# A one-core convolution kernel: the tap coefficients reordered by small copies instead of a matmul, and the start-up work dealt out anew

## The chip, the cores and the metric

One core of a Trainium2 chip runs the kernel. The metric is the device time of one execution in microseconds (us), lower is better, taken as the median of several executions. The engines are TensorE (PE for its matmuls, PEld for its weight loads), VectorE (DVE), ScalarE (ACT), GpSimd (POOL) and SyncE (SP, which here only issues transfers). Each engine works through its own queue in order; they meet only at semaphores.

## The reference

The input x is 8 images of 32 channels, 64 by 64, in float32. It is normalised per channel and image (32 groups of one channel). The four pixels of each 2 by 2 square become four channel blocks, 128 channels in all, in the order (row parity, column parity) = 00, 01, 10, 11. Three depthwise convolutions of width 1, 3 and 5 give 384 feature channels, `w_proj` (128 by 384) mixes them into 128, these are put back into the 2 by 2 squares, and x is added.

```
xd    = concat(x[:, :, 0::2, 0::2], x[:, :, 0::2, 1::2], x[:, :, 1::2, 0::2], x[:, :, 1::2, 1::2])   # x normalised
feats = concat(dwconv(xd, w1, 1), dwconv(xd, w3, 3), dwconv(xd, w5, 5))
y     = einsum('bchw,oc->bohw', feats, w_proj[:, :, 0, 0])
out   = x + un-deinterleave(y)
```

## The kernel before

The 25 taps of the widest convolution fall into an inner square of 9 and a ring of 16. For an inner tap the three convolutions and the projection are folded into one effective 128 by 128 weight: `weff[n] = w5(n) * wp5^T + w3(n) * wp3^T`, and for the centre also `w1 * wp1^T`. These run on PE. Each weight and each image is split into a high half that PE's fast float32 form holds exactly (`whi`, `HI`) and a remainder (`wlo`, `LO`), and each image takes three passes over its nine taps: `whi` by `HI`, `wlo` by `HI`, `whi` by `LO`, 18 matmuls each of up to 512 columns. The ring runs on the other engines: DVE accumulates its taps in `ACC` (L645, L649), ACT makes further products in `PROD` (L476) and POOL adds them into `RING_SUM` (L343); DVE joins the two in `F` (L661), and PE multiplies `F` by `wpT`, the transposed third part of w_proj (L778, for the last image L788). A last stage adds x and stores. The images follow each other without a gap, and each engine's order is written out by hand.

The change touches the start, in which weights and the statistics of image 0 are made ready:

- The partitions hold the channels in a permuted order (column parity before row parity). w_proj lands in `wp_sb`; ACT permutes its three parts, last one first (L408, semaphore `permuted`); PE transposes them with a permuted identity, `ident_ph` (L795), and ACT copies the third part to `wpT` (L412).
- The 35 coefficients of each channel (25 of w5, 9 of w3, 1 of w1) land in `w_sb` in the reference's order. PE multiplies them by `ident_ph` (L698), which permutes the partitions, and ACT copies the result to `coef` (L414 for the first 34, L494 for w1's).
- The effective weights: ACT scales taps 0 to 2, and after its first HI piece taps 3 and 4 (L420); POOL scales taps 5 to 8 (L358); DVE adds w3's part of each (L600) and w1's part of tap 8 (L631). POOL casts taps 0 to 2 to `whi` (L365), DVE taps 3 to 5 and 6 to 8 (L608); POOL makes `wlo` in three steps (L374).
- The statistics of image 0: DVE takes them in quarters from `XS` (L552), spreads them (L613); PE sums over partitions (`sum_parts`, L705); DVE aggregates (L557) and adds epsilon (L559); POOL raises to the power -1/2 (L312, `inv_std`); DVE makes the bias `nbias` (L564, `part_bias`).
- With these, ACT makes the even columns of the first 17 rows of `HI` of image 0 (L428) and DVE the odd ones (L623). ACT goes on with the other rows and then with `G`, the plain normalised image (L438), on which the ring starts.
- PE runs matmuls on zeros before its work, `WARM[0]` of 256 columns and `WARM[1]` of 512 (L691). Image 0's first pass goes in chunks of three taps; a bank is half an image. It needs `hi_top` (both pieces of HI) and each chunk's `whi`.

Of the kernel before, what the change touches and what calls it, by code (L numbers as in the profile page):

```python
# [6 lines left out]
ACT = mybir.ActivationFunctionType  # L7
# [6 lines left out]
P = 4 * C  # L14
# [36 lines left out]
WARM = (20, 5)  # L51
WARM_COLS = 256
CHUNK = 3
CHUNKS = N_INNER // CHUNK
ACT_SCALED = 5
# [45 lines left out]
def build(nc, x, w1, w3, w5, wp, out):  # L101
    with ExitStack() as ctx:  # L102
# [6 lines left out]
        def sem(name):  # L109
            return ctx.enter_context(nc.semaphore(name))  # L110
# [42 lines left out]
        COEF_PS = SMALL[:, 200:200 + N_COEF]  # L153
# [7 lines left out]
        wp_loaded, w_loaded, w1_loaded = sem("wp_loaded"), sem("w_loaded"), sem("w1_loaded")  # L161
        coef_ready, coef_copied = sem("coef_ready"), sem("coef_copied")
# [83 lines left out]


# [36 lines left out]
        def _(pool):  # L284
# [24 lines left out]
            def inv_std(n, a, b):  # L309
                pool.wait_ge(mhalf_ready, 1)  # L310
                pool.wait_ge(stat_step, n)
                pool.tensor_tensor(rstd[:, a:b], vare[:, a:b], mhalf[:, a:b], ALU.pow).then_inc(rstd_done, 1)  # L312
# [44 lines left out]
            def scale_w5(n):  # L357
                pool.tensor_scalar(weff[:, n, :], wpT[:, :], of5(INNER[n]), None, ALU.mult).then_inc(pool_scaled, 1)  # L358

            inv_std(1, 0, 1)  # L360
            pool.wait_ge(wpT_ready, 1)
            pool.wait_ge(coef_copied, 1)
            scale_w5(ACT_SCALED)
            pool.wait_ge(weff_step, CHUNK)
            pool.tensor_copy(whi[:, 0:CHUNK, :], weff[:, 0:CHUNK, :]).then_inc(whi0_ready, 1)  # L365
            for n in range(ACT_SCALED + 1, N_INNER):
                scale_w5(n)
            for k in range(CHUNKS):
                taps = slice(k * CHUNK, (k + 1) * CHUNK)
                if k == 0:  # L370
                    pool.wait_ge(whi0_ready, 1)
                else:
                    pool.wait_ge(whi_ready, k)
                pool.tensor_tensor(wlo[:, taps, :], weff[:, taps, :],  # L374
                                   whi[:, taps, :].bitcast(F32), ALU.subtract).then_inc(wlo_ready, 1)
# [24 lines left out]
        def _(act):  # L400
            load_parts(act, 0, 512, 1024, xs_loaded[1])
            act.dma_start(w_sb[:, 0:W3_AT], w5.rearrange("c a h w -> c (a h w)")).then_inc(w_loaded, 16)
            act.dma_start(w_sb[:, W3_AT:W1_AT], w3.rearrange("c a h w -> c (a h w)")).then_inc(w_loaded, 16)
# [8 lines left out]
            act.activation(wpT[:, :], WT_PS[:, 2 * P:3 * P], ACT.Copy).then_inc(wpT_ready, 1)  # L412
            act.wait_ge(coef_ready, 1)
            act.activation(coef[:, 0:W1_AT], COEF_PS[:, 0:W1_AT], ACT.Copy).then_inc(coef_copied, 1)  # L414
            act.wait_ge(wpT_ready, 1)
            act.wait_ge(coef_copied, 1)

            def scale_w5(n0, n1):
                for n in range(n0, n1):
                    act.activation(weff[:, n, :], wpT[:, :], ACT.Copy,  # L420
                                   scale=of5(INNER[n])).then_inc(w5_scaled, 1)

            scale_w5(0, CHUNK)
# [68 lines left out]
            scale_w5(CHUNK, ACT_SCALED)  # L492
            act.wait_ge(coef_ready, 2)
            act.activation(coef[:, W1_AT:N_COEF], COEF_PS[:, W1_AT:N_COEF], ACT.Copy).then_inc(coef_copied, 1)  # L494
# [29 lines left out]
        def _(dve):  # L524
# [29 lines left out]
            def part_variance(b):  # L554

                dve.wait_ge(spread_summed, b + 1)
                dve.bn_aggr(agg1[:, b, :], SPREAD_PS[b]).then_inc(agg1_done, 1)  # L557
                dve.wait_ge(agg1_done, b + 1)
                dve.tensor_scalar(vare[:, b:b + 1], agg1[:, b, 1:2], EPS, None, ALU.add).then_inc(stat_step, 1)  # L559
# [44 lines left out]
            def cast_w(k):  # L604
# [9 lines left out]
                              mask[:, :, None].to_broadcast([P, PARTS, STATS]), ALU.mult).then_inc(spread_done, 1)  # L614
            part_variance(0)
            dve.wait_ge(wt_ready, 1)
            dve.wait_ge(coef_copied, 1)
            part_bias(0)
            add_w3(0, 1, 2)
# [6 lines left out]
            add_w3(3, 4, 5)  # L626
# [3 lines left out]
            dve.wait_ge(coef_copied, 2)  # L630
# [54 lines left out]
        def _(pe):  # L685
# [11 lines left out]
            def coefficients(c0, c1):  # L697
                nc.tensor.matmul(COEF_PS[:, c0:c1], ident_ph[:, :], w_sb[:, c0:c1],  # L698
                                 start=True, stop=True).then_inc(coef_ready, 1)

            def sum_parts(b):
                pe.wait_ge(spread_done, b + 1)
                if b == 0:
                    pe.wait_ge(stat_const, PARTS + 1)
                nc.tensor.matmul(SPREAD_PS[b], same[:, :], spread[:, b, :, :].rearrange("p k s -> p (k s)"),  # L705
                                 start=True, stop=True).then_inc(spread_summed, 1)
# [83 lines left out]

            sum_parts(0)
            pe.wait_ge(ident_permuted, 1)
            for n, k in enumerate((2, 1, 0)):
                pe.wait_ge(permuted, n + 1)
                mm = nc.tensor.transpose(WT_PS[:, k * P:(k + 1) * P], wp_ph[:, k, :], ident_ph[:, :])  # L795
            mm.then_inc(wt_ready, 1)
            pe.wait_ge(w_loaded, 32)
            coefficients(0, W1_AT)
# [3 lines left out]
            pe.wait_ge(w1_loaded, 16)  # L802
            pe.wait_ge(coef_copied, 1)
            coefficients(W1_AT, N_COEF)
# [26 lines left out]
```

## Time and profile before

| | |
|---|---|
| median of 3 executions | 135.5 us (135.26 to 136.7) |
| the profiled execution | 135.7 us, of which the profile's span is 133.9 us |
| busy in the span | PE 124.9 us (93%), DVE 125.0 (93%), POOL 119.9 (90%), ACT 110.3 (82%) |
| granted TensorE clock | 0.986 of full speed over the span |

The span runs from the first to the last instruction of the profiled execution; 1.8 us of the execution lie outside it. A busy engine is not yet a late one: what sets the end is seen from the chain of waits and from the order of time in the stage that is changed.

### The profile page before, as it was taken

How to read it: one execution, taken by the hardware profiler on the slowest of the kernel's cores; microseconds unless marked ns; L12 is line 12 of the kernel's file. 1: busy time of each engine (PE TensorE's matmuls, PEld its weight loads, DVE VectorE, ACT ScalarE, POOL GpSimd, SP SyncE). 2: the span in 40 equal slices, each digit the busy share in tenths (PEclk: the TensorE clock that was granted, in tenths of full speed). 3: DMA queues.
4: the chain of work that ended last, by engine and by line, in shares of the span. 5: the costliest groups of instructions: out<-in, count | busy, mean ns of one | idle time of the engine just before them, and what ended most of it. 6: DMA issues, size and time to landing. Idle time of an engine off the chain costs nothing.

```text
span 133.9 us, 1668 instructions
## 1 busy us (share of the span) xinstructions
PE 124.9 (93%) x514; PEld 96.8 (72%) x514; DVE 125.0 (93%) x234; ACT 110.3 (82%) x116; POOL 119.9 (90%) x92
## 2 busy tenths in 40 slices
PE   6968999999999999999999999999999999999910
PEld 6955788888886887688886888688877688578700
DVE  6679999999979999999999999999999999999960
ACT  2389979999999999999999999999999999160010
POOL 6269879999999999999999999999999999999970
PEclk9999999999999999999999999999999999999995
DMA  4999999880044008097979873989299919897876
GB/s 136 260 250 201 207 209 201 169 167 0 5 81 81 0 0 161 5 117 95 187 115 117 155 168 39 91 144 190 30 100 134 186 37 115 91 110 145 182 159 143
DMA packets 35944, 16.68 MB, mean 125 GB/s; under 512 B 34144, under 2 KB 34272, under 8 KB 35552
## 3 DMA queue, kind: packets, MB, share of 16 engines
q0 software_dynamic: 1488, 6.93, 38.8%
q1 hardware_dynamic: 32784, 9.11, 35.6%
q10 hardware_dynamic: 1664, 0.54, 1.7%
q8 instruction: 4, 0.07, 0.2%
q14 instruction: 4, 0.03, 0.1%
HBM read 5.46 MB, written 4.19 MB: 72 GB/s over the span
## 4 chain that ended last, share of the span: by engine, by line
POOL 62%; issue 16%; DVE 12%; PE 4%; POOLq 1%; ACT 1%; ACTq 0%
POOL RING_SUM L343 56%; DVE ACC L649 4%; POOL X L393 3%; PE YP L691 3%; POOL LO L330 2%; DVE st L546 2%; DVE weff L600 2%; DVE whi L608 1%; POOLq L102 1%; DVE ACC L645 1%; DVE stp L552 1%; DVE HI L623 1%; PE YP L795 1%; POOL rstd L312 0%; POOL wlo L385 0%
## 5 line engine op out<-in xcount | busy, mean ns | idle before, releaser
L343 POOL TENSOR_TENSOR RING_SUM<-RING_SUM,PROD 128x900 f32<-128x900 f32 (+1 forms) x45 | 93.0, 2072 | 3.4
L649 DVE SCALAR_TENSOR_TENSOR ACC<-G,coef,ACC 128x480 f32<-128x480 f32 (+3 forms) x132 | 82.4, 742 | 0.0
L476 ACT ACTIVATE PROD<-G,coef 128x900 f32<-128x900 f32 (+1 forms) x45 | 44.5, 1051 | 0.0
L723 PE MATMUL YP<-HI,wlo 128*128 128x512 f32 (+1 forms) x146 | 38.1, 412 | 0.0
L723 PE MATMUL YP<-HI,whi 128*128 128x512 f32 (+1 forms) x146 | 36.2, 398 | 1.7 <-DVE HI L623 1.2
L723 PE MATMUL YP<-LO,whi 128*128 128x512 f32 (+1 forms) x146 | 36.0, 398 | 0.0
L723 PEld LDWEIGHTS YP<-HI,wlo 128*128 128x128 f32 x146 | 27.5, 189 | 8.6 <-issue 2.9
L723 PEld LDWEIGHTS YP<-HI,whi 128*128 128x128 f32 x146 | 27.2, 189 | 8.7 <-DVE HI L623 1.3
L723 PEld LDWEIGHTS YP<-LO,whi 128*128 128x128 f32 x146 | 27.5, 189 | 6.7 <-issue 0.5
L438 ACT ACTIVATE G<-X,nbias,rstd 64x1024 f32<-64x1024 f32 x16 | 21.1, 1321 | 1.2 <-DVE nbias L564 0.9
L459 ACT ACTIVATE Y<-YP 64x1024 f32<-64x1024 f32 x14 | 15.4, 1097 | 3.4 <-PE YP L778 3.1
L778 PE MATMUL YP<-F,wpT 128*128 128x512 f32 x28 | 13.3, 596 | 0.0
L645 DVE TENSOR_SCALAR ACC<-G,coef 128x512 f32<-128x512 f32 x16 | 11.5, 781 | 0.0
L661 DVE TENSOR_TENSOR F<-ACC,RING_SUM 128x512 f32<-128x512 f32 (+1 forms) x18 | 10.7, 672 | 0.0
L467 ACT ACTIVATE RING_SUM<-G,coef 128x1024 f32<-128x1024 f32 x8 | 9.2, 1145 | 0.1
L778 PEld LDWEIGHTS YP<-F,wpT 128*128 128x128 f32 x28 | 5.2, 189 | 4.3 <-issue 3.4
L447 ACT ACTIVATE HI<-G 128x1024 fp32r<-128x1024 f32 x7 | 7.4, 1062 | 0.2
L449 ACT ACTIVATE LO<-HI 128x1024 fp32r<-128x1024 f32 x7 | 7.4, 1062 | 0.2
L546 DVE BATCH_NORM_STATS2 st<-X 128x6 f32<-128x512 f32 x12 | 7.4, 681 | 0.0
L691 PE MATMUL YP<-LO 128*128 128x256 f32 (+1 forms) x25 | 6.1, 423 | 1.2 <-DVE LO L526 1.2
L513 ACT ACTIVATE Y<-YP 64x256 f32<-64x256 f32 x2 | 0.8, 406 | 7.2 <-PE YP L788 7.2
L330 POOL DMA_DIRECT2D LO<-G x7 | 6.4, 914 | 0.0
(69 smaller groups left out, 66.4 us busy)
## 6 DMA issues: line engine op xcount, KB each, us to landing
LO<-G POOLq DMA_DIRECT2D x7, 527.5 KB, 5.3
X<-in_x_dram SPq DMA_DIRECT2D x14, 256.0 KB, 5.5
X<-Y POOLq DMA_DIRECT2D x6, 512.0 KB, 7.3
out_dram<-X SPq DMA_DIRECT2D x12, 256.0 KB, 4.5
XS<-in_x_dram SPq DMA_DIRECT2D x1, 512.0 KB, 6.1
out_dram<-X SPq DMA_DIRECT2D x4, 128.0 KB, 2.2
X<-in_x_dram SPq DMA_DIRECT2D x2, 136.0 KB, 4.4
XS<-in_x_dram SPq DMA_DIRECT2D x1, 256.0 KB, 3.3
```

The costliest lines, as they stand in the source:

```text
L343: pool.tensor_tensor(dst, dst, prod(b, k), ALU.add).then_inc(prod_added, 1)
L438: act.activation(g_image(b, r0, r1)[HALF * j:HALF * (j + 1)], rows[:, :, :, j], ACT.Identity, bias=nbias[p0:p0 + HALF, col(b):col(b) + 1], ...
L459: act.activation(Y[p0:p0 + HALF, b // 2 % 2, :, :, j], YP[HALF * j:HALF * (j + 1), b % AREAS, :].rearrange("p (h w) -> p h w", w=PW), ACT. ...
L467: act.activation(RING_SUM[:, b % SUMS, :, :], g_tap(b, POOL_OF[b][0], True), ACT.Copy, scale=of5(POOL_OF[b][0])).then_inc(first_prod, 1)
L476: act.activation(prod(b, k), g_tap(b, POOL_OF[b][k + 1]), ACT.Copy, scale=of5(POOL_OF[b][k + 1])).then_inc(prod_ready, 1)
L546: dve.bn_stats(st[:, t, q, :], rows).then_inc(bn_done, 1)
L645: dve.tensor_scalar(ACC[:, h * BANK_ROWS:(h + 1) * BANK_ROWS, :], half_tap(b, tap, h, True), of5(tap), None, ALU.mult).then_inc(acc_half[h ...
L649: dve.scalar_tensor_tensor(half_part(ACC, tap, h), half_tap(b, tap, h), of5(tap), half_part(ACC, tap, h), ALU.mult, ALU.add).then_inc(acc_ ...
L661: dve.tensor_tensor(F[:, b % 2, rows.start * PW:rows.stop * PW].rearrange("p (h w) -> p h w", w=PW), ACC[:, rows, :], RING_SUM[:, b % SUMS ...
L691: nc.tensor.matmul(YP[:, 0, 0:n], zeros[:, 0:P], zeros[:, 0:n], start=True, stop=True)
L723: mm = nc.tensor.matmul(dst, w[:, n, :], src, start=start, stop=False, skip_group_check=True)
L778: mm = nc.tensor.matmul(YP[:, b % AREAS, cols], wpT[:, :], F[:, b % 2, cols], start=False, stop=True, skip_group_check=True)
```

## The change

- `w_sb` is no longer permuted on PE. DVE copies w5's 25 columns in four blocks of 32 partitions to `coef`, then w3's nine in four blocks; POOL copies w1's column in four blocks, each of which waits for the one before. Three semaphores (`coef5`, `coef3`, `coef1`) take the place of two. PE's two coefficient matmuls and ACT's two copies of them are gone.
- PE transposes the third part of w_proj ahead of `sum_parts`, into the bank `SMALL`, and the other two behind it. ACT can copy `wpT` after the first.
- ACT scales taps 0 to 6, all ahead of its first HI piece; POOL scales taps 7 and 8.
- DVE adds w3 to taps 0 and 1 before `part_variance(0)`, to 2 and 3 before `part_bias(0)`, to 4 and 5 after its HI piece. POOL scales its first tap before it waits for the variance, and copies w1's column between its last tap and the first `wlo`.
- `WARM[0]` is 17 instead of 20.

```diff
-WARM = (20, 5)
+WARM = (17, 5)
-ACT_SCALED = 5
+ACT_SCALED = 7
+        def in_order(c0, c1, block):
+            src = (block % 2) * 2 + block // 2
+            return coef[C * block:C * (block + 1), c0:c1], w_sb[C * src:C * (src + 1), c0:c1]
...
 # POOL
-            inv_std(1, 0, 1)
             pool.wait_ge(wpT_ready, 1)
-            pool.wait_ge(coef_copied, 1)
+            pool.wait_ge(coef5, 4)
             scale_w5(ACT_SCALED)
+            inv_std(1, 0, 1)
             pool.wait_ge(weff_step, CHUNK)
             pool.tensor_copy(whi[:, 0:CHUNK, :], weff[:, 0:CHUNK, :]).then_inc(whi0_ready, 1)
             for n in range(ACT_SCALED + 1, N_INNER):
                 scale_w5(n)
+            pool.wait_ge(w1_loaded, 16)
+            for block in range(PARTS):
+                if block == 0:
+                    pool.wait_ge(pool_scaled, N_INNER - ACT_SCALED)
+                else:
+                    pool.wait_ge(coef1, block)
+                to, of = in_order(W1_AT, N_COEF, block)
+                pool.tensor_copy(to, of).then_inc(coef1, 1)
+            pool.wait_ge(coef1, PARTS)
...
 # ACT
             act.wait_ge(wt_ready, 1)
-            act.activation(wpT[:, :], WT_PS[:, 2 * P:3 * P], ACT.Copy).then_inc(wpT_ready, 1)
-            act.wait_ge(coef_ready, 1)
-            act.activation(coef[:, 0:W1_AT], COEF_PS[:, 0:W1_AT], ACT.Copy).then_inc(coef_copied, 1)
+            act.activation(wpT[:, :], SMALL[:, 0:P], ACT.Copy).then_inc(wpT_ready, 1)
             act.wait_ge(wpT_ready, 1)
-            act.wait_ge(coef_copied, 1)
+            act.wait_ge(coef5, 4)
-            scale_w5(0, CHUNK)
+            scale_w5(0, ACT_SCALED)
...
             high_half(0, TOP, 0, hi_top)
-            scale_w5(CHUNK, ACT_SCALED)
-            act.wait_ge(coef_ready, 2)
-            act.activation(coef[:, W1_AT:N_COEF], COEF_PS[:, W1_AT:N_COEF], ACT.Copy).then_inc(coef_copied, 1)
...
 # DVE
+            dve.wait_ge(w5_loaded, 16)
+            for block in range(PARTS):
+                to, of = in_order(0, W3_AT, block)
+                dve.tensor_copy(to, of).then_inc(coef5, 1)
+            dve.wait_ge(w3_loaded, 16)
+            for block in range(PARTS):
+                to, of = in_order(W3_AT, W1_AT, block)
+                dve.tensor_copy(to, of).then_inc(coef3, 1)
+            dve.wait_ge(wt_ready, 2)
+            dve.wait_ge(coef3, PARTS)
+            add_w3(0, 1)
             part_variance(0)
-            dve.wait_ge(wt_ready, 1)
-            dve.wait_ge(coef_copied, 1)
+            add_w3(2, 3)
             part_bias(0)
-            add_w3(0, 1, 2)
             dve.wait_ge(stats_ready, 1)
...
-            add_w3(3, 4, 5)
+            add_w3(4, 5)
             cast_w(1)
             add_w3(6, 7, 8)
             dve.wait_ge(weff_step, N_INNER)
-            dve.wait_ge(coef_copied, 2)
+            dve.wait_ge(coef1, PARTS)
...
 # PE
+            pe.wait_ge(ident_permuted, 1)
+            transpose(2, SMALL[:, 0:P]).then_inc(wt_ready, 1)
             sum_parts(0)
-            pe.wait_ge(ident_permuted, 1)
-            for n, k in enumerate((2, 1, 0)):
-                pe.wait_ge(permuted, n + 1)
-                mm = nc.tensor.transpose(WT_PS[:, k * P:(k + 1) * P], wp_ph[:, k, :], ident_ph[:, :])
-            mm.then_inc(wt_ready, 1)
-            pe.wait_ge(w_loaded, 32)
-            coefficients(0, W1_AT)
+            transpose(1, WT_PS[:, P:2 * P])
+            transpose(0, WT_PS[:, 0:P]).then_inc(wt_ready, 1)
             pe.wait_ge(low_zero, 2)
             for _ in range(WARM[1]):
                 keep_warm(512)
-            pe.wait_ge(w1_loaded, 16)
-            pe.wait_ge(coef_copied, 1)
-            coefficients(W1_AT, N_COEF)
```

## Rows read from the trace of the kernel before

**Rows 1.** Chain that ended last, two pieces: start us, length us, what.
```profile
24.87 0.52 POOL rstd L312
...
123.73 4.65 POOL X L393 x2
```

**Rows 2.** Timeline of the end: start us, busy us, engine, line, operation, count, idle before.
```profile
125.19 1.49 DVE L661 TENSOR_TENSOR F<-ACC,RING_SUM 128x256 f32<-128x256 f32 x4
125.74 1.59 PEld L788 LDWEIGHTS YP<-F,wpT 128*128 128x128 f32 x8 [0.31 <-DVE F L661]
```

**Rows 3.** Timeline of DVE, 5 to 15 us.
```profile
5.33 0.21 DVE L613 TENSOR_TENSOR spread<-stp,mask 128x48 f32<-128x48 f32 x1
6.30 0.38 DVE L557 BATCH_NORM_AGGREGATE agg<-YP 128x2 f32<-128x48 f32 x1 [0.75 <-PE YP L705]
...
7.72 0.21 DVE L564 TENSOR_SCALAR nbias<-agg,rstd 128x1 f32<-128x1 f32 x1 [0.86 <-POOL rstd L312]
7.97 0.94 DVE L600 SCALAR_TENSOR_TENSOR weff<-YP,coef,weff 128x128 f32<-128x128 f32 x3
8.94 0.83 DVE L623 TENSOR_SCALAR HI<-X,rstd,nbias 64x544 fp32r<-64x544 f32 x1
...
10.70 0.49 DVE L608 CAST whi<-weff 128x384 fp32r<-128x384 f32 x1
...
12.39 1.13 DVE L608 CAST whi<-weff 128x384 fp32r<-128x384 f32 x1
...
14.64 1.39 DVE L645 TENSOR_SCALAR ACC<-G,coef 128x512 f32<-128x512 f32 x2
```

**Rows 4.** Timeline of PE, 0 to 11 us.
```profile
1.17 4.63 PE L691 MATMUL YP<-LO 128*128 128x256 f32 x20 [1.17 <-DVE LO L526]
...
6.06 0.87 PE L795 MATMUL YP<-ident_ph,wp_ph 128*128 128x128 f32 x3
...
7.01 1.46 PE L691 MATMUL YP<-LO 128*128 128x512 f32 x5
...
9.82 0.97 PE L723 MATMUL YP<-HI,whi 128*128 128x512 f32 x3 [1.25 <-DVE HI L623]
```

**Rows 5.** Timeline of ACT, 4 to 15 us.
```profile
4.92 0.71 ACT L408 ACTIVATE wp_ph<-wp_sb 128x128 f32<-128x128 f32 x3 [0.97 <-DMA wp_sb<-in_L_conv_w_proj_dram]
6.96 0.28 ACT L412 ACTIVATE wpT<-YP 128x128 f32<-128x128 f32 x1 [1.34 <-PE YP L795]
...
7.53 0.99 ACT L420 ACTIVATE weff<-wpT,coef 128x128 f32<-128x128 f32 x3
8.43 0.87 ACT L428 ACTIVATE HI<-X,nbias,rstd 64x544 fp32r<-64x544 f32 x1
9.19 0.69 ACT L420 ACTIVATE weff<-wpT,coef 128x128 f32<-128x128 f32 x2
...
11.50 2.67 ACT L438 ACTIVATE G<-X,nbias,rstd 64x1024 f32<-64x1024 f32 x2
```

**Rows 6.** Timeline of POOL, 7 to 14 us.
```profile
7.02 0.56 POOL L312 TENSOR_TENSOR rstd<-vare,mhalf 128x1 f32<-128x1 f32 x1 [2.51 <-DVE vare L559]
...
8.97 0.50 POOL L365 CAST whi<-weff 128x384 fp32r<-128x384 f32 x1 [0.74 <-DVE weff L600]
9.46 1.88 POOL L358 TENSOR_SCALAR weff<-wpT,coef 128x128 f32<-128x128 f32 x3
11.31 1.99 POOL L374 TENSOR_TENSOR wlo<-weff,whi 128x384 fp32r<-128x384 f32 x2
```

**Rows 7.** Small instructions: a step of the chain on DVE (128x1), POOL's timeline.
```profile
24.20 0.07 DVE dev L575
```
```profile
1.44 1.67 POOL L294 TENSOR_SCALAR_AFFINE_SELECT same<-same 128x128 f32<-128x128 f32 x4
```

**Rows 8.** Transfers of w3's coefficients: the issue on ACT's queue; KB and us to landing.
```profile
1.66 0.45 ACTq L403 DMA_DIRECT2D w_sb<-in_L_conv_w_dram  x1
```
```profile
w_sb<-in_L_conv_w_dram ACTq DMA_DIRECT2D x1, 4.5 KB, 4.1
```

More of the change, by code:

```diff
@@ L152, in build @@
         WT_PS, SMALL = YP[:, 2, 0:512], YP[:, 2, 512:1024]
-        COEF_PS = SMALL[:, 200:200 + N_COEF]
         SPREAD_PS = [YP[:, 1, 512 * n:512 * n + PARTS * STATS] for n in range(2)]
@@ L160, in build @@
         xs_loaded = [sem(f"xs_loaded{n}") for n in range(3)]
-        wp_loaded, w_loaded, w1_loaded = sem("wp_loaded"), sem("w_loaded"), sem("w1_loaded")
-        coef_ready, coef_copied = sem("coef_ready"), sem("coef_copied")
+        wp_loaded, w5_loaded, w3_loaded, w1_loaded = sem("wp_loaded"), sem("w5_loaded"), sem("w3_loaded"), sem("w1_loaded")
+        coef5, coef3, coef1 = sem("coef5"), sem("coef3"), sem("coef1")
         stat_const, part_stats, spread_done = sem("stat_const"), sem("part_stats"), sem("spread_done")
@@ L358, in scale_w5 @@
                 pool.tensor_scalar(weff[:, n, :], wpT[:, :], of5(INNER[n]), None, ALU.mult).then_inc(pool_scaled, 1)
+            pool.wait_ge(wpT_ready, 1)
+            pool.wait_ge(coef5, 4)
+            scale_w5(ACT_SCALED)
             inv_std(1, 0, 1)
-            pool.wait_ge(wpT_ready, 1)
-            pool.wait_ge(coef_copied, 1)
-            scale_w5(ACT_SCALED)
             pool.wait_ge(weff_step, CHUNK)
@@ L401, in _ @@
             load_parts(act, 0, 512, 1024, xs_loaded[1])
-            act.dma_start(w_sb[:, 0:W3_AT], w5.rearrange("c a h w -> c (a h w)")).then_inc(w_loaded, 16)
-            act.dma_start(w_sb[:, W3_AT:W1_AT], w3.rearrange("c a h w -> c (a h w)")).then_inc(w_loaded, 16)
+            act.dma_start(w_sb[:, 0:W3_AT], w5.rearrange("c a h w -> c (a h w)")).then_inc(w5_loaded, 16)
+            act.dma_start(w_sb[:, W3_AT:W1_AT], w3.rearrange("c a h w -> c (a h w)")).then_inc(w3_loaded, 16)
             act.dma_start(w_sb[:, W1_AT:N_COEF], w1.rearrange("c a h w -> c (a h w)")).then_inc(w1_loaded, 16)
@@ L695, in _, with transpose @@
                 keep_warm(WARM_COLS)
-            def coefficients(c0, c1):
-                nc.tensor.matmul(COEF_PS[:, c0:c1], ident_ph[:, :], w_sb[:, c0:c1],
-                                 start=True, stop=True).then_inc(coef_ready, 1)
+            def transpose(k, dst):
+                pe.wait_ge(permuted, 3 - k)
+                return nc.tensor.transpose(dst, wp_ph[:, k, :], ident_ph[:, :])
             def sum_parts(b):
```

## The prediction

> **What bounds the kernel now.** I read the chain of waits first. Its last piece of work is POOL's final addition, from 123.73 to 128.38 us, and behind 24.87 us, where POOL takes the second images' variance from DVE, it stays on POOL [rows 1]. So POOL is its own bound from there on, and what starts it is DVE. The end of the timeline shows that the others are level with it: DVE makes the last F from 125.19 us, and PE waits only 0.31 us for it [rows 2]. Three engines are full to the end, within a few tenths of each other. The start-up therefore counts in full, but only what moves DVE's first ring instruction, at 14.64 us [rows 3], moves the end: DVE runs from it without a gap worth the name, and POOL is started from DVE's statistics. For PE the question is how late it may start: it had about 0.3 us to spare at the end.
>
> Then I read the start in order of time, one engine after another. The first stage belongs to image 0's statistics: spread at 5.33, aggregate at 6.30 (after 0.75 us of waiting for PE), bias at 7.72 (after 0.86 us of waiting for POOL), HI at 8.94, and the two casts at 10.70 and 12.39 [rows 3]. The two waits are room on DVE. ACT goes from wpT at 6.96 to its taps at 7.53 and starts HI at 8.43, then has two more taps at 9.19 before it goes on to HI and G [rows 5]. PE's first real matmul, at 9.82, waited 1.25 us for DVE's HI piece [rows 4], which had begun at 8.94 and taken 0.83 [rows 3].
>
> **The change part by part.** All times are forecast positions in the profiled execution.
>
> *wpT.* The third part of w_proj is permuted first: three permutations took 0.71 us from 4.92, 0.30 for one, so it is there at 5.22 [rows 5]. PE's zeros took 4.63 us for 20, 0.23 each [rows 4]; with 17 they end at about 5.1 and stand in nobody's way. In the row of the transposes three took 0.87 us; each starts about 0.22 after the one before, and the last is 0.42 long [rows 4]. With 0.2 for its weight load, the first one is out at about 5.25 + 0.20 + 0.42 = 5.9. ACT's copy, 0.28 us [rows 5], then ends at 6.2 where it ended at 7.24: 1.04 us gained for wpT.
>
> *DVE's eight copies.* DVE is free at 5.54 [rows 3], w5 landed before that, and w3 at 1.66 + 4.1 = 5.76 [rows 8]. No copy of 32 partitions stands in the trace. The nearest row from below is the 128x1 subtraction, a step of 0.07 us in the chain [rows 7]; from above it is the aggregate, 0.38 us for 48 elements [rows 3]. I take 0.10, near the lower one, since 25 and 9 elements add little to one: coef5 complete at about 5.95 and coef3 at 6.35. At the lower end they are complete at 5.85 and 6.1, at the upper end (0.2, half the aggregate, since neighbours overlap) at 6.35 and 7.15. The removed matmul and ACT's copies give back about 0.3 us between wpT and the first tap (7.24 to 7.53 [rows 5]): the first tap now starts at about 6.25.
>
> *The statistics are pushed back.* This is the term against the change. In DVE's queue two w3 additions and the wait for the other two transposes stand ahead of `part_variance(0)`, and behind that POOL's power, the bias, and both HI pieces. PE has `sum_parts` behind the first transpose, which costs it about 0.1, and two transposes behind that: done at about 6.8 (before, three were done at 6.06 + 0.87 = 6.93 [rows 4]). The addition itself is 0.94 us for three, 0.32 apart [rows 3]. So additions at 6.85 and 7.17 (tap 1 is scaled by 6.25 + 0.3 + 0.4 = 6.95), aggregate at 7.5 instead of 6.30. From the aggregate to the bias it was 7.72 - 6.30 = 1.42 us [rows 3], through POOL's 0.56 [rows 6]: now the bias starts at 8.9, ends at 9.1. POOL's own order adds nothing, since its first tap (1.88 / 3 = 0.63 us [rows 6]) fits between 6.25 and 8.1.
>
> *HI.* Before, DVE had three additions between bias and HI: 7.72 to 8.94 [rows 3]. Now only the bias itself stands there: HI at 9.15 instead of 8.94, done at 9.98. ACT's piece was ready to start at 8.43; now its seven taps (0.30 apart: three and the step to HI took 7.53 to 8.43 [rows 5]) end at about 8.4 and it waits for the bias until 9.13: piece done at 10.0. PE's first matmul thus comes at about 10.0 instead of 9.82, 0.2 late. That is no loss in the end, as its second chunk waits for the cast at 10.70 in any case, plus the cast's 0.49 [rows 3].
>
> *Behind HI.* ACT saves the two taps (0.69 us [rows 5]) and the last coefficient; it is at G at about 11.6 (before 11.50), and G is done at 14.3, so the later start has eaten the whole saving. DVE has two additions instead of three ahead of its first cast: 9.98 + 0.64 = 10.64 against 10.70. It gains 0.05 us.
>
> *POOL.* After the power (done at 8.8) come the cast of 0.50, one tap of 0.63 instead of three of 1.88 [rows 6], then the four copies of w1's column, each waiting for the last. The row with that pattern is the four selects of 1.67 us [rows 7]: 0.42 each at 128 elements. Without the elements I take 0.27, the bounds being 0.1 and 0.42: 1.1 us, 0.4 to 1.7. The first wlo then starts at 9.95 + 1.1 = 11.1 (10.4 to 11.7) against 11.31 [rows 6]. What hides the copies is the tap work taken from POOL; without that cover they would delay wlo by their 1.1 us.
>
> *The second cast.* It took 1.13 us where the first one of the same shape took 0.49 [rows 3], and it ended just after POOL's two wlo, 11.31 + 1.99 = 13.30 [rows 6]. I take it that it is held up by wlo: now 11.1 + 2.0 = 13.1, cast done at about 13.35 against 13.52, 0.1 to 0.2 earlier. After two statistics instructions DVE's ring starts at 14.5, behind G at 14.3.
> The Trainium skill, "GPSIMD Engine Reference", section "8. Key points", says that GpSimd shares its SBUF interfaces with VectorE and contends with its two-port perf modes. The pair of 0.49 and 1.13 us agrees; if it were not so, the cast would take 0.49 again, and the gain would be bounded by G, as in the second rival.
>
> *Sum.* On the path that sets the end: -0.05 at the first cast, -0.1 at the second, 0 for ACT, 0 for PE's late start. That is -0.1 us against the profiled execution, 135.7, which itself stands 0.2 above the median. I apply it to the median: 135.5 - 0.1 = 135.4 us. With the unknown costs at their ends: copies of 0.2 on DVE push the aggregate from 7.5 to about 7.9 and everything behind by 0.4 (+0.3); copies of 0.42 on POOL put the second wlo at 13.7 and the cast at 13.9 (+0.4); both at their low ends, G stops the gain at -0.3.
>
> **The rivals.** About 1% (1.4 us) is what a measurement of this kernel can tell from no change.
>
> *The push-back of the statistics wins.* Chance 0.17. If the copies take 0.2 each and POOL's 0.42 each, the aggregate, HI, the first cast and the first wlo all move by 0.3 to 0.6: 135.5 + 0.6 = 136.1 us. For it speaks that four waits now stand in one row ahead of the bias. Against it, 0.07 us steps on DVE.
>
> *The statistics hardly move and the relief of DVE and POOL shows.* Chance 0.22. If the transposes come sooner than I think, and the POOL copies take 0.1, wlo begins before 10.5, the second cast is free of it, and only G's 14.3 or sooner holds DVE back: 135.5 - 0.4 = 135.1 us.
>
> *TensorE's clock.* Chance 0.08, and it is the one that ends slower by over 1%. The first zeros have 256 columns in 0.23 us, the later ones 512 in 1.46 / 5 = 0.29 us or less [rows 4]: the first run at the lower of the two levels, 1.2 GHz, the later ones at 2.4. The rise happened between 5.8 and 7.1 us (the end of the first, the second of the later ones), after PE had been busy since 1.17. In the new kernel PE has three zeros less, a small gap before the first transpose, and after its last zeros, at about 8.2 instead of 8.6, nothing until 10.0: 1.8 us idle where the row shows 1.25 behind a last small matmul. If the level fell there, a 512-column matmul would take about 0.2 us more (0.46 at the first pace, against 0.29 or less); for 11 of them 2.2 us, less the 0.4 us between PE's first three matmuls (done at 10.79 [rows 4]) and the first cast (done at 11.19 [rows 3]), in which PE waits anyway, and less the 0.3 it has to spare at the end [rows 2]: +1.5, 137.0 us. It decides from four slow matmuls on, and for over 1% from 11. Against it: the level did not fall in the gap of the kernel before.
> The Trainium skill, "TensorE: Matmul & The Clock Gate", section "HAM oscillation — how this bites in real kernels", describes a clock that falls back in waits between bursts of matmuls; the gap in this trace did not do it.
>
> *The freed engines meet otherwise later on*, in a way that gains over 1%: chance 0.04; nothing in the rows speaks for it. The change may be undone entirely by the order of the other engines, which is the forecast's own case.
>
> **How the numbers follow.** The forecast has 0.49, the others 0.17, 0.22, 0.08 and 0.04. The first three all lie within 1%: 0.88, less 0.02 for a bad sum of both late cases, 0.86. Slower by over 1%: 0.08 + 0.02 = 0.10; faster 0.04. The range is from the second rival, 135.1, less 0.3 of spread between executions, to the first, 136.1, and 0.4 more for the same reason and for a short stretch of low clock: 134.8 to 136.5.
>
> **What would show it.** In the new profile: wpT copied at about 5.9, the first tap at 6.25; the eight copies between 5.5 and 6.4; aggregate at 7.5, bias at 8.9, both HI pieces from 9.1; PE's first real matmul at 10.0; first cast at 10.65; POOL's four copies over 1.1 us and wlo from 11.1; second cast done by 13.4 and DVE's ring from 14.5. The forecast is wrong if the bias comes before 8.5 or after 9.3, if ring and casts don't move together, or if matmuls of image 0 take twice as long.

## The result and the profile after

The changed kernel is slower: a median of 136.83 us (135.84 to 138.45, 20 executions) against 135.54 us (135.13 to 136.70, 20 executions) of the kernel before on the same chips. The recorded ratio is 1.0063 with a 95% interval of 1.0037 to 1.0088; it leaves out executions far above a kernel's fastest (here the one of 138.45 us), and it is not the ratio of the medians, which is 1.0095 with that execution and 1.0092 without it. The loss is thus 0.6 to 0.95%. The times also lie wider: 12 of 20 stand above 136.5 us, where it was four of 20. The profiled execution took 136.73 us, its span 134.9 us.

The start of the new kernel on DVE, which answers to [rows 3], in order of time:

```profile
5.59 0.77 DVE L626 COPY coef<-w_sb 32x25 f32<-32x25 f32 x4
6.39 0.80 DVE L630 COPY coef<-w_sb 32x9 f32<-32x9 f32 x4
7.30 0.61 DVE L608 SCALAR_TENSOR_TENSOR weff<-YP,coef,weff 128x128 f32<-128x128 f32 x2
7.82 0.37 DVE L565 BATCH_NORM_AGGREGATE agg<-YP 128x2 f32<-128x48 f32 x1
...
9.14 0.21 DVE L572 TENSOR_SCALAR nbias<-agg,rstd 128x1 f32<-128x1 f32 x1 [0.25 <-POOL rstd L316]
9.39 0.83 DVE L640 TENSOR_SCALAR HI<-X,rstd,nbias 64x544 fp32r<-64x544 f32 x1
...
10.90 0.36 DVE L616 CAST whi<-weff 128x384 fp32r<-128x384 f32 x1
...
12.46 1.12 DVE L616 CAST whi<-weff 128x384 fp32r<-128x384 f32 x1
...
14.70 1.39 DVE L662 TENSOR_SCALAR ACC<-G,coef 128x512 f32<-128x512 f32 x2
...
17.81 0.38 DVE L565 BATCH_NORM_AGGREGATE agg<-YP 128x2 f32<-128x48 f32 x1 [0.51 <-PE YP L723]
```

DVE's ring starts 0.06 us later than before, not 0.14 earlier. The new thing is the last line: DVE now waits 0.51 us for PE's sum over image 1's statistics. The kernel before had no such wait:

```profile
17.15 0.37 DVE L557 BATCH_NORM_AGGREGATE agg<-YP 128x2 f32<-128x48 f32 x1
```

The same on PE (answers to [rows 4]), ACT [rows 5] and POOL [rows 6]:

```profile
1.17 3.99 PE L708 MATMUL YP<-LO 128*128 128x256 f32 x17 [1.17 <-DVE LO L534]
5.44 0.45 PE L717 MATMUL YP<-ident_ph,wp_ph 128*128 128x128 f32 x1 [0.28 <-ACT wp_ph L421]
...
6.50 2.48 PE L708 MATMUL YP<-LO 128*128 128x512 f32 x5
10.40 5.80 PE L741 MATMUL YP<-HI,whi 128*128 128x512 f32 x18 [1.43 <-ACT HI L439]
16.05 1.58 PE L741 MATMUL YP<-HI,wlo 128*128 128x512 f32 x6
```
```profile
5.93 0.28 ACT L425 ACTIVATE wpT<-YP 128x128 f32<-128x128 f32 x1 [0.23 <-PE YP L717]
6.46 2.15 ACT L431 ACTIVATE weff<-wpT,coef 128x128 f32<-128x128 f32 x7 [0.26 <-DVE coef L626]
9.47 2.46 ACT L439 ACTIVATE HI<-X,nbias,rstd 64x544 fp32r<-64x544 f32 x3 [0.85 <-DVE nbias L572]
11.95 2.69 ACT L449 ACTIVATE G<-X,nbias,rstd 64x1024 f32<-64x1024 f32 x2
```
```profile
10.32 0.99 POOL L379 COPY coef<-w_sb 32x1 f32<-32x1 f32 x4 [0.15 <-POOL weff L362]
11.39 1.97 POOL L387 TENSOR_TENSOR wlo<-weff,whi 128x384 fp32r<-128x384 f32 x2
```

PE is the surprise. Its five zeros of 512 columns take 2.48 us where they took 1.46, and the 18 matmuls of the first pass run without a wait and still end with `wlo` starting at 16.05 us. Before, they began at 9.82, waited twice for casts, and the `wlo` matmuls began 0.97 us sooner:

```profile
15.08 1.58 PE L723 MATMUL YP<-HI,wlo 128*128 128x512 f32 x6
```

Why shows in the lengths of PE's weight loads, all of the same 128x128 weights. The groups of the line of the tap matmuls, first of the kernel before from 9.5 to 13.3 us, then of the new kernel from 10.3 to 13.3 and from 15 to 20 us (nanoseconds min/median/max, then first and last start):

```profile
L723 PEld LDWEIGHTS YP<-HI,whi x12: 186/188/192, 9.8 to 13.0; 128*128 128x128 f32 x12
```
```profile
L741 PEld LDWEIGHTS YP<-HI,whi x8: 288/330/333, 10.4 to 13.1; 128*128 128x128 f32 x8
L741 PE MATMUL YP<-HI,whi x7: 594/602/795, 10.4 to 13.1; 128*128 128x512 f32 x4, 128*128 128x480 f32 x3
...
L741 PEld LDWEIGHTS YP<-HI,wlo x18: 187/188/192, 15.8 to 20.0; 128*128 128x128 f32 x18
```

330 ns is TensorE at the lower of its two levels, 1.2 GHz, and 188 ns is TensorE at 2.4 GHz: in the profile of e5, below, the same loads have a median of 332 ns where the granted clock reads 0.50, and of 188 ns behind it, where it reads 1.00. In this execution the level rose only at about 13.4 us, three microseconds into the convolution.

A second difference stands on POOL, between 31 and 36 us:

```profile
29.59 3.96 POOL L347 TENSOR_TENSOR RING_SUM<-RING_SUM,PROD 128x930 f32<-128x930 f32 x2
34.04 4.08 POOL L347 TENSOR_TENSOR RING_SUM<-RING_SUM,PROD 128x900 f32<-128x900 f32 x2 [0.49 <-POOL RING_SUM L347]
```

POOL idles 0.49 us between two additions of one chain, put down to POOL itself, where the usual step between two such additions is 0.14. In the kernel before:

```profile
30.65 6.20 POOL L343 TENSOR_TENSOR RING_SUM<-RING_SUM,PROD 128x900 f32<-128x900 f32 x3
```

In the chain of waits POOL's final addition starts at 124.97 us instead of 123.73 [rows 1]. That chain runs through ACT from 19.75 to 108.91 us and only then through POOL, so it doesn't tell by itself what the pause costs. The start times of the same additions in the two profiles do. POOL's are 0.67 us later than before from image 1's statistics on, 0.91 us from 26.2 us on, and 1.27 us from the pause on, and stay at 1.22 to 1.30 to the end. ACT's instructions from image 1 on are 0.64 to 0.74 us later. The first two steps come from PE: image 1's aggregate starts at 17.81 instead of 17.15 us, and the next variance, which needs another sum from PE, 0.91 us later:

```profile
24.54 0.15 DVE L581 TENSOR_TENSOR vare<-dev,YP 128x1 f32<-128x1 f32 x1
```
```profile
25.45 0.16 DVE L589 TENSOR_TENSOR vare<-dev,YP 128x1 f32<-128x1 f32 x1
```

### The profile page after: what moved, and what is told of

Same layout as the page of the kernel before. It is cut to its first block, busy times and chain, and to the rows that moved or that the text cites. A ratio compares the mean times of both kernels' runs of the same rounds, so it can differ in the third digit from the quotient of the medians.

```text
span 134.9 us, 1665 instructions
## 1 busy us (share of the span) xinstructions
PE 126.0 (93%) x507; PEld 97.1 (72%) x507; DVE 126.2 (94%) x242; ACT 110.9 (82%) x116; POOL 119.4 (88%) x94
## 4 chain that ended last, share of the span: by engine, by line
ACT 60%; POOL 15%; issue 8%; PE 5%; DVE 2%; POOLq 1%; ACTq 0%
ACT PROD L487 27%; ACT G L449 14%; POOL RING_SUM L347 11%; ACT HI L458 6%; PE YP L741 5%; ACT LO L460 5%; ACT Y L470 4%; ACT RING_SUM L478 4%; POOL X L406 3%; POOLq L102 1%; DVE ACC L666 1%; ACT HI L439 1%; DVE agg L565 1%; DVE weff L608 0%; POOL rstd L316 0%
## 5 line engine op out<-in xcount | busy, mean ns | idle before, releaser
L741 PE MATMUL YP<-HI,whi 128*128 128x512 f32 (+1 forms) x146 | 37.0, 408 | 1.4 <-ACT HI L439 1.4
L741 PEld LDWEIGHTS YP<-HI,whi 128*128 128x128 f32 x146 | 28.5, 196 | 8.7 <-ACT HI L439 2.1
L796 PE MATMUL YP<-F,wpT 128*128 128x512 f32 x28 | 13.3, 596 | 0.2 <-DVE F L678 0.2
L678 DVE TENSOR_TENSOR F<-ACC,RING_SUM 128x512 f32<-128x512 f32 (+1 forms) x18 | 10.4, 621 | 0.0
```

Of the source, the lines that this page charges most:

```text
L678: dve.tensor_tensor(F[:, b % 2, rows.start * PW:rows.stop * PW].rearrange("p (h w) -> p h w", w=PW), ACC[:, rows, :], RING_SUM[:, b % SUMS ...
L741: mm = nc.tensor.matmul(dst, w[:, n, :], src, start=start, stop=False, skip_group_check=True)
L796: mm = nc.tensor.matmul(YP[:, b % AREAS, cols], wpT[:, :], F[:, b % 2, cols], start=False, stop=True, skip_group_check=True)
```

## The experiments

Each kernel ran on one chip with the kernel before beside it, 10 to 12 executions of its own. Medians are compared, with the share of executions above 136.5 us, and the ratio to the kernel before with its interval. Fifteen kernels were run: e1 to e4 on one chip, e5 to e12 on a second, e13 to e15 on a third. The changed kernel itself was not run beside them, so a difference from its 136.83 us can also hold a difference between chips.

**e1, e2: more zeros ahead of the first convolution.**

```
e1:  changed kernel,  -WARM = (17, 5)   +WARM = (17, 9)
e2:  kernel before,   -WARM = (20, 5)   +WARM = (20, 8)
```

> The changed kernel with nine matmuls on zeros of 512 columns instead of five between the transposes and the first convolution. Theory A (the clock): in the changed kernel PE stands idle from 8.98 to 10.40 us and its first matmuls run at the lower level, with weight loads of 330 ns instead of 188; with four zeros more PE is busy up to about 10 us, the level rises before the first convolution or at the latest in it, the first pass of image 0 ends 0.5 to 1 us sooner and the median falls from about 136.8 to 135.9 to 136.3 us. Theory B (the later statistics alone): PE still starts at 10.4 us, and nothing else changes: 136.8 us within 0.2.

> The kernel before with eight zeros of 512 columns instead of five. Theory A: its own executions of 136.5 to 136.7 us (five of 20) are those in which the clock rises late; with the gap before the first convolution filled they get rarer, and the median goes to 135.3 or 135.4. Theory B: no change of the spread; the coefficient matmul behind the zeros comes up to 0.7 us later, which costs 0 to 0.2 us.

e1: 136.48 us, 5 of 12 above 136.5; ratio 1.0060 (1.0025 to 1.0094). e2: 135.48 us, 3 of 12 above; ratio 0.9968 (0.9941 to 0.9996). Both medians moved the way of the clock theory (theory A), but by less than it asked for: e1 by 0.35 us, its ratio hardly at all, and the long executions of e2 (137.57 to 139.94 us) are no rarer than the five of 35 above 136.5 of the kernel before beside it. The profile of e1 caught an execution of 137.81 us whose first pass was at full level, with `wlo` matmuls from 14.90 us although the convolution began only at 10.14: a late start alone costs PE nothing. What was slow there is another place, told at the end.

**e3, e11: is it the three zeros taken away?**

```
e3:  kernel before,   -WARM = (20, 5)   +WARM = (17, 5)
e11: changed kernel,  -WARM = (17, 5)   +WARM = (20, 5)
```

> The kernel before with 17 zeros instead of 20 at the start, nothing else. Theory A: three zeros less make PE's early activity thinner, so the clock rises late in more executions: a median 0.3 to 1.0 us above that of before. Theory B: the zeros only bridge time; same as before within 0.15 us.

> The changed kernel with 20 zeros at the start as before, nothing else. Theory A by way of the three zeros taken away: the median falls by 0.3 to 0.6 us, from 136.8 to 136.2 to 136.5. If it is the later start of the convolution (the gap of PE in the middle) and not the three zeros that matters, the median stays within 0.2 us of 136.8.

e3: 135.93 us, 0.28 above the kernel before beside it, ratio 1.0024 (0.9997 to 1.0052), not told apart from no change and between the two theories. Its profile, of an execution of 136.39 us, does show the cold pass: the level fell at 11.44 us behind an idle stretch of 1.52 us, and the `wlo` matmuls began at 15.87 instead of 15.08 us. e11: 137.06 us, 11 of 12 above 136.5, ratio 1.0099 (1.0068 to 1.0131). Giving the three zeros back to the changed kernel showed no gain; it is the slowest of all. PE's timeline of e11:

```profile
6.27 1.41 PE L708 MATMUL YP<-LO 128*128 128x512 f32 x5
10.53 5.96 PE L741 MATMUL YP<-HI,whi 128*128 128x512 f32 x18 [2.85 <-ACT HI L439]
```

With the level up early the five zeros are over at 7.68 us, PE idles 2.85 us, and the level falls again at 10.82 us, just behind the start of the 18 matmuls. So the cold pass comes in two ways. In the profiles of the changed kernel, e4 and e12 the level has not risen before the convolution at all: the five zeros are slow, and the idle stretch is 1.43, 0.79 and 0.79 us. In those of e3, e5 and e11 it has risen and falls back at 10.4 to 11.4 us, with idle stretches of 1.52, 2.27 and 2.85 us. The length of the idle stretch alone doesn't tell the cases apart: e1 idles 1.90 us and e7 1.71 us behind nine zeros, and both stay at full level. What the three early zeros are worth by themselves stays open.

**e4: the statistics of image 0 in the old order.** POOL's power ahead of its first tap, and on DVE:

```
 dve: w5's copies
-     w3's copies; wait wt_ready 2, coef3; add_w3(0, 1); part_variance(0); add_w3(2, 3); part_bias(0)
+     part_variance(0); w3's copies; wait wt_ready 2, coef3; part_bias(0); add_w3(0, 1, 2)
 dve: HI piece; add_w3(3, 4, 5) instead of (4, 5)
```

> The changed kernel with the statistics of image 0 in the old order: variance directly behind w5's copies, POOL's power ahead of its first tap, all three additions between bias and HI. Theory B (the push-back of the statistics is what costs): the aggregate comes at about 6.5 instead of 7.82, both HI pieces by 9.5, PE starts at 9.5 instead of 10.4, and the median falls by 0.5 to 0.8 us. Theory A (the clock): PE still has its gap of idle and the cold start; the clock's rise is not moved, and the median falls by at most 0.3 us.

136.60 us, 7 of 12 above 136.5; ratio 1.0054 (1.0024 to 1.0084). The places moved as expected (aggregate at 6.48, PE's first real matmul at 9.81 us), the time by 0.2 us only. In its profile the 18 matmuls took 6.11 us, ten of their weight loads were slow, and the `wlo` matmuls began at 15.77 us: in that execution the clock ate what the order gave back.

**e5, e6: the gap in POOL's stream.** Small memsets to a scratch column, at 3.1 us, where POOL has time:

```
             pool.memset(mhalf[:, :], -0.5).then_inc(mhalf_ready, 1)
+            for n in range(N):
+                pool.memset(scratch[:, n:n + 1], 0.0)
e5: changed kernel, N = 1      e6: kernel before, N = 4
```

> The changed kernel with one memset of a 128x1 scratch column more in POOL's queue, at 3.1 us, where POOL is idle. Theory C (position in POOL's instruction stream): in the changed kernel POOL stands still for 0.46 us at 33.58 us between the semaphore it waited for and the next addition, with all its inputs there; in the kernel before the same 0.44 us stand at the same count of instructions (before the 68th), but behind a running addition, where they cost nothing. One instruction more shifts that place under the running addition: the gap is gone from the idle time, the variance of images 4 to 7 comes 0.4 us sooner, and the median falls by 0.35 to 0.5 us. Theory D (the gap belongs to data, as a product of ScalarE that is late): the gap stays, and the time is that of the changed kernel within 0.15 us (136.2 us where the clock was undisturbed).

> The kernel before with four such memsets, which is how many instructions the change adds to POOL's queue. Theory C: the gap of 0.46 us opens between the semaphore and the addition as in the changed kernel, and the median rises by 0.35 to 0.5 us, to about 135.9. Theory D: nothing but 0.1 us of idle POOL time is used; same as before within 0.15 us.

POOL's timeline of e5, then of e6, in the same stretch:

```profile
29.66 8.20 POOL L350 TENSOR_TENSOR RING_SUM<-RING_SUM,PROD 128x930 f32<-128x930 f32 x4
```
```profile
28.19 3.94 POOL L346 TENSOR_TENSOR RING_SUM<-RING_SUM,PROD 128x930 f32<-128x930 f32 x2
32.63 4.09 POOL L346 TENSOR_TENSOR RING_SUM<-RING_SUM,PROD 128x900 f32<-128x900 f32 x2 [0.50 <-POOL RING_SUM L346]
```

One idle memset more and the four additions of the changed kernel follow each other without a gap; four memsets in the kernel before and a gap of 0.50 us is there. No product and no semaphore differs, so the gap belongs to a place in POOL's instruction stream. The trace has it ahead of the same record by count in the changed kernel, e1, e4, e6, e11 and e13; in the kernel before that record is a semaphore at 35.32 us, reached while an addition is running, and there it costs nothing. In time: e6 135.95 us, +0.33 by the medians, ratio 1.0021 (0.9993 to 1.0049); the time alone doesn't settle it, the profile does. e5: 136.79 us, 9 of 10 above 136.5, ratio 1.0078 (1.0045 to 1.0112): no gain in the median, against the 0.35 to 0.5 us that were expected. These nine have a granted clock of 0.962 to 0.984 over their span, the tenth, of 135.77 us, has 0.994, so the clock hides here what the memset is worth; why so many executions met it is open. The profile shows one of them, in the busy times by stretches (PE, PEld, DVE, ACT, POOL, then granted clock, DMA share, GB/s):

```profile
6.95:10.35 3.40, 1.13 (x6) 0.59 (x4) 2.95 (x10) 2.55 (x8) 1.88 (x5) 1.00 1.15 222
10.40:13.75 3.35, 3.35 (x8) 2.75 (x9) 3.25 (x9) 3.27 (x4) 2.78 (x7) 0.50 1.26 188
13.80:20.00 6.20, 6.20 (x29) 5.09 (x28) 5.49 (x12) 4.92 (x6) 4.47 (x5) 1.00 1.21 206
```

PE was busy 1.13 of 3.40 us ahead of the convolution, and the granted clock stands at 0.50 for the first 3.35 us of it.

**e7, e8: the remedies put together.**

```
e7: e1 and the memset of e5
e8: e7 and the order of e4
```

> The changed kernel with the one memset and nine zeros of 512 columns. Theory A (cold clock) and C together make up the loss: undisturbed executions at 135.4 to 135.6 us, as the kernel before, median 135.5 to 136.0. If something else is lost too (the late statistics, the copies), undisturbed executions stay above 135.8.

> The same with the statistics in the old order. If A and C are the whole loss, what is left of the change is the gain of DVE's start: its first ring instruction at 14.5 instead of 14.64 us, so 0.1 to 0.2 us below the kernel before in undisturbed executions (135.2 to 135.4). If the late statistics cost by themselves, it is 0.4 to 0.6 us faster than the one before it in this list; else within 0.2 us of it.

e7: 135.93 us, 3 of 12 above 136.5; ratio 1.0035 (1.0007 to 1.0062). e8: 135.58 us, 4 of 12; ratio 1.0016 (0.9987 to 1.0044), six executions between 135.3 and 135.56. By the medians the order of the statistics was worth 0.35 us here, but the executions of the two kernels overlap widely; e14 and e15 below settle it. In the two profiles, both at full level, DVE's ring starts at 14.58 us in e7 and at 14.25 in e8.

**e9, e10, e12: the rest of PE's idle stretch.** Four zeros more, issued when the bias is there, so that they fill the time in which the HI pieces are made:

```
                 keep_warm(512)
+            pe.wait_ge(stats_ready, 1)
+            for _ in range(4):
+                keep_warm(512)
e9: e8 with this   e10: e2 with this, behind coefficients(W1_AT, N_COEF)   e12: e8 with WARM = (17, 5)
```

> The kernel with the memset, nine zeros and the statistics in the old order, and four more zeros of 512 columns issued once the bias of image 0 is there, which fill PE's last idle stretch before the first convolution. Theory A (the clock falls or rises late because of PE's idle time ahead of the first convolution): the slow executions of 136.5 us and more, four of 12 without these zeros, get rarer; median 135.3 to 135.5. If what is left of them comes from another place (a load of an image that lands late), their share stays at a quarter or a third.

> The kernel before with eight zeros, and four more once the bias is there. Theory A: fewer slow executions than before's quarter, median 135.2 to 135.5, and no change of the undisturbed ones. Rival: the late zeros hold up the first convolution by up to 0.2 us, and the median is that of before or above.

> The changed kernel with the memset and the statistics in the old order, but only five zeros: against the kernel with nine it shows what four zeros are worth. Theory A: median 136.0 to 136.4, that is 0.4 to 0.8 us above the one with nine, while its fastest executions are the same, 135.3 to 135.4. Rival (the order of the statistics is what matters and zeros do nothing): the same median within 0.2 us, 135.6.

| memset, old order of the statistics | median us | range | above 136.5 |
|---|---|---|---|
| 5 zeros (e12) | 136.00 | 135.32 to 136.84 | 1 of 12 |
| 9 zeros (e8) | 135.58 | 135.30 to 138.89 | 4 of 12 |
| 9 and 4 zeros (e9) | 135.44 | 135.25 to 135.98 | 0 of 12 |

e12 has six of 12 above 136.2, e9 none. The medians of neighbouring rows overlap too widely to be told apart; the range of e9 is what differs. e10: 135.69 us (135.29 to 136.21), none above 136.5, ratio 0.9978 (0.9946 to 1.0009), while the kernel before beside it reached 137.09. Its median is not below the 135.61 of that kernel, as the rival had it: in its profile the late zeros hold the convolution up until 10.18 us. PE's timeline of e9:

```profile
6.33 3.35 PE L710 MATMUL YP<-LO 128*128 128x512 f32 x13
9.60 0.96 PE L743 MATMUL YP<-HI,whi 128*128 128x512 f32 x3
```

In the profiles the count of zeros and the cold pass go together. Of the eight kernels with five zeros of 512 columns, six have eight to ten slow weight loads in the first pass and two none (the kernel before and e6). The nine with eight zeros or more have none.

**e13, e14, e15: one remedy at a time, with the clock out of the way.**

```
e13: e1 and the late zeros   e14: e13 and the memset   e15: e9 again
```

> The changed kernel with its own order of the statistics and without the memset, with nine zeros and four more once the bias is there: PE's idle stretch before the first convolution is filled, nothing else. Theory A (the clock is the larger part of the loss): the executions above 136.7 us go, and the median falls from 136.8 to 135.9 to 136.1, where the gap in POOL's stream and the late statistics are left. Rival (the late statistics are the larger part): the median stays above 136.4.

> The same with the one memset in POOL's queue. Theory C: 0.2 to 0.45 us below the one without it, at 135.6 to 135.8. What is left above the kernel with the old order of the statistics (135.44 us) is what the late statistics cost: 0.1 to 0.3 us. Rival: no difference from the one without the memset, within 0.1 us.

> The best version once more (memset, statistics in the old order, nine and four zeros), for a tighter comparison with the kernel before: 135.4 us within 0.15, 0.1 to 0.3% below before by the medians; no execution above 136.2.

| step | median us | difference | ratio to before |
|---|---|---|---|
| the changed kernel | 136.83 | | 1.0063 (1.0037 to 1.0088) |
| + zeros over the idle stretch (e13) | 136.11 | -0.72 | 1.0029 (1.0005 to 1.0053) |
| + one memset (e14) | 135.75 | -0.36 | 1.0002 (0.9977 to 1.0026) |
| + old order of the statistics (e15; e9 135.44) | 135.42 | -0.33 | 0.9993 (0.9969 to 1.0016) |

The three kernels of this list ran on one chip, the first line on others; by the ratios the first step is 0.0034, or 0.46 us, so its part is 0.5 to 0.7 us. The other two steps stand on one chip: of the 12 executions each, 11 of e14 lie at or below 135.99 us and eight of e13 above it, and 11 of e14 lie at or above 135.65 and ten of e15 below it. The ratios put the last step at 0.12 us only. No execution of e13 and e14 stands above 136.5 us, one of e15 does, against the expectation. In the last step DVE's ring starts sooner (e14 first, then e9):

```profile
14.75 1.39 DVE L665 TENSOR_SCALAR ACC<-G,coef 128x512 f32<-128x512 f32 x2
```
```profile
14.31 1.39 DVE L664 TENSOR_SCALAR ACC<-G,coef 128x512 f32<-128x512 f32 x2
```

The 0.44 us between these two lines is too much for the order alone, since e14's profile caught slow zeros (see the end); the two clean profiles of e7 and e8 are 0.33 us apart, those of e13 and e15 0.13 (14.50 and 14.37 us). The best version is 0.16 us below the kernel before by the medians (135.42 against 135.58), which its interval doesn't tell from no change.

## Why the prediction was wrong

The forecast was 135.4 us, range 134.8 to 136.5; it came to 136.83 and the other sign.

**The step that failed** is "That is no loss in the end", on PE's later first matmul, the term "0 for PE's late start". It was argued from data alone: the second chunk waits for its cast in any case. On that it was right: with the level up (e1's profile) PE began at 10.14 us and lost nothing. But in more than half of the executions, as far as their times tell, the first pass ran partly at the lower level: the clock had not risen yet, or it fell back behind the idle stretch. I had this as the rival "TensorE's clock" and gave it 0.08, on the ground that "the level did not fall in the gap of the kernel before". One profiled execution can't say that: the kernel before has it too. Of its 132 executions beside the experiments, 26 have a granted clock of 0.971 to 0.974 over the span, and none of them takes less than 136.20 us (median 136.52); the other 106, with 0.983 or more, have a median of 135.55. The rival had the level fall in the gap, which e3, e5 and e11 show; in the profile of the changed kernel it had not risen yet, which comes to the same for the first pass. The price of one slow matmul was right too: the rival's own sum, with the eight slow weight loads of the profile in place of 11, gives 8 x 0.2 - 0.4 - 0.3 = 0.9 us, and the variance at 25.45 us is 0.91 late. Over all executions the part is 0.5 to 0.7 us. The chance was far too low, as 12 of 20 executions stand above 136.5 us.

The path was wrong too. The sentence "only what moves DVE's first ring instruction [...] moves the end", with 0.3 us for PE to spare at the end, left out that DVE needs PE's sums for the statistics of the next images. The ring's start moved by 0.06 us, image 1's aggregate by 0.66. The chain of waits of the changed kernel has it: PE from 10.40 to 17.62, then DVE's aggregate of image 1.

```profile
10.40 7.22 PE YP L741 x24
17.62 0.17 PE YP L723 x2
...
17.81 0.39 DVE agg L565
```

With that the term is +0.5 to +0.7 us in the median instead of 0.

**A term that was not in the sum at all**: four records more in POOL's stream ahead of the same addition (four copies and their waits, less two taps) move a pause from under a running addition into the open. It costs 0.49 us instead of the usual 0.14 in the profile, and 0.36 us by the medians of e13 and e14. I had counted POOL's copies by their time, and that was right (1.1 us forecast, 0.99 measured), but not by their number. In the profile of before nothing of it can be read off the idle times, as it was covered.

**The statistics' push-back** was seen as "the term against the change", but taken as balanced by DVE's and ACT's savings. Its size was off: the copies cost 0.20 us each, not 0.10 (0.77 and 0.80 us for four), the value I had as the upper bound. So two additions began at 7.30 instead of 6.85, aggregate 7.82 (7.5), bias 9.14 (8.9), HI 9.39 (9.15), first cast 10.90 (10.65; the prediction's 9.98 + 0.64 is 10.62, not 10.64), `wlo` 11.39 (11.1), second cast done at 13.58 (13.35), ring 14.70 us (14.5). From the bias on a shift of about 0.25 us runs through unchanged, close to the +0.3 that the sum had for copies of 0.2 us. The rival "The push-back of the statistics wins" had this half of its condition right and the other wrong, as POOL's copies took 0.25 us each and not 0.42; its price was +0.6, and e14 and e15 show 0.33 by the medians, 0.12 by the ratios. Part of the lateness, 0.14 us at the statistics' first instruction, is this execution's transfers.

**What held**: wpT copied at 5.93 us (forecast 5.9), the second cast of 1.12 us beside 0.36 for the first, held up again until POOL's `wlo` was over, and ACT gaining nothing because it waits for the bias (0.85 us). Of the three signs that were to show the forecast wrong, the bias (9.14 us) and the ring with the casts stayed within bounds; the third came in part, with matmuls of 602 instead of 400 ns (medians).

**The gain that was meant** is not shown: with all three losses taken back the kernel stands 0.16 us below before by the medians, within the interval. Against the kernel before with the same kind of zeros (e10, on the chip of e9) it is 0.25 us by the medians and nothing by the ratios.

## What to carry to other kernels

Where TensorE has a stretch without work ahead of its first real matmuls, look at several executions and at the lengths of its weight loads, not at one profile: an edit that only shifts the work ahead of them by some tenths changed the level of the first pass in about every second execution here. More zeros, the last ones released by the semaphore of the data that the real work waits for, took it away here; they can also hold the real work up. When instructions are added to a queue that is the bound for the rest of the kernel, compare the gaps of that queue late in the kernel as well, and try one idle instruction more before putting a loss of a few tenths down to the work itself.

## What the runs showed of the hardware that was not expected

- The granted clock column reads 1.00 ahead of the first rise, whatever the level: five zeros took 1.46 us at the one and 2.48 us at the other with the same 1.00 beside them. The lengths of the weight loads (188 against 330 ns) tell the level there.
- Filling the stretch has its own cost where the level is low: in e14's profiled execution the 13 zeros took 5.02 us and held the convolution up until 11.37 us, in an execution of 136.25 us against a median of 135.75.
- Behind a late image transfer the level fell in mid-kernel. In e1's profile DVE waited for the statistics' input, PE for DVE, and the clock fell (longest waits, then the stretch of 3.3 us):

```profile
DVE st L554 <- DMA X<-in_x_dram: 2.2, 2, 1.7
...
PE YP L729 <- DVE agg L577: 1.7, 1, 1.7
```
```profile
36.00:39.30 3.30, 3.30 (x10) 2.64 (x9) 3.23 (x11) 3.30 (x4) 3.30 (x4) 0.50 0.10 20
```

  DVE's statistics meet their transfers with little to spare at that place; e8 waited 0.71 us there. Moving them later was not tried.
- What the pause of 0.44 to 0.50 us in POOL's stream is, was not settled. Shown is that in these kernels it keeps its place by the count of records ahead of it, with zeros and order changed.
